# Graph network of four residual layers: source scales on GpSimd, chunk sums by an identity product and ScalarE

## Chip, cores and metric

The kernel runs on one core of a Trainium2 chip. The metric is the device time of one execution in microseconds (us), the median of several.

## What is computed

6250 nodes with 128 features, 206250 edges (sorted by destination, self loops among them), and four layers, each followed by `x = layernorm(x + layer(x))`:

```python
xw = x @ W0; ew = edge_attr @ edge_w
x = ln(x + segment_sum(xw[src] * ew, dst) + b0)                 # layer 0
agg = segment_sum(x[src], dst) / max(deg, 1)
x = ln(x + agg @ W_l.T + b_l + x @ W_r.T)                       # layer 1
norm = rsqrt(deg_src + eps)[src] * rsqrt(deg_dst + eps)[dst]
x = ln(x + segment_sum(x[src] * norm, dst) @ W2 + b2)           # layer 2
# layer 3: GCN sum, tanh, sigmoid gate, batch norm over all nodes
```

## The kernel before

Nodes lie in NB = 49 blocks of 128. A **loop** over 202 steps (about 95 to 2100 us) works through the edges: GpSimd gathers rows of `xw` by edge, TensorE and VectorE form layer 0's messages and sum them by node, and beside it TensorE and VectorE build the adjacency matrix, which is kept in DRAM as 196 float16 slices of 32 destinations each (`at`). As soon as blocks of layer 0 are final, the loop also normalises them, stores them as high and low float16 halves (`parts_v`, in `yT`), and already sums layer 1's neighbours with them: `acc` (which lies in `y`) holds features x destinations, in NCK = 14 **chunks** of CD = 448 columns. At the loop's end `DONE[c]` source blocks are in chunk c: 42, 45, 42, 42, 42, 42, 41, 42, 42, 42, 45, 45, 45, 45. The last NL = 4 blocks (LB = 45 on) are normalised only behind the loop.

The **stretch behind the loop** (2100 to 2164 us) finishes layer 1, and all that the change touches lies in it. There are two sizes: the 14 chunks c of 448 columns, and NCH = 13 chunks q of CB = 4 blocks (512 columns, the last one 128). `needs(q)` is the number of chunks c that q spans: 2, 3, 4, 5, 6, 7, 8, 10, 11, 12, 13, 14, 14.

- **TensorE** (`last_products`, L1489 on): for chunk c the products that are missing, two (high and low) for each source block from `DONE[c]` to 49, into PSUM bank `LAST_BANK[c % 4]`. Chunks 0 to 3 do the blocks below 45 first (18 products), then come the transposes and linear products of the last four blocks (L1520 to L1525), then chunks 0 to 13 to the end. Behind chunk c = `needs(q)` stands `y_linear(q)` (L1503): it waits for `needs(q)` chunks in `acc` and multiplies four blocks by the weights.
- **VectorE** (L1062 to L1122): `sum_out(i)` adds the bank of chunk i to `acc`. Between these stand the turns: turn q has `y_out(q)` (L1072, scale and add into `x`), `y_stats(q-1)` (L1081, L1085), `y_norm(q-2)` (L1093, L1095), `y_scaled(q-3)` (L1102: normalised rows times `src_l2` into `xs_c`) and `y_low(q-4)` (L1107: the low half for layer 2).
- **ScalarE** (L1752 on): turn q has the root for q (L1756), the normalised rows of q-1 into `y` (L1761, four instructions), and the cast of `xs_c` of q-2 to the high half (L1767).
- **GpSimd** (L781 on), done with its gathers: it adds layer 2's bias to `y`, chunk by chunk, once `xs_c` of the chunk is written (L784).
- **SyncE** loads the last adjacency pieces of each chunk c (L414) and the first chunks of the dense part (`chunk_in`, L429): the first waits for the ninth finished piece, the second for the fourteenth.

The **dense part** follows (layers 2 and 3, to the end): TensorE multiplies the halves of all 49 blocks by each adjacency chunk (`main`, L1569 and L1570). In its first chunk it waits before every fourth block b for `y_low(b // 4)`. Ahead of it TensorE has to be through with all `y_linear`, with a loaded flag and with a branch. All engines run their own queues in the order in which the program is written, tied by semaphores; there is no scheduler.

Of the kernel before, what the change touches and what calls it, by code (L numbers as in the profile page):

```python
# [16 lines left out]
ALU = mybir.AluOpType  # L17
# [5 lines left out]
D = 128  # L23
ED = 16
P = 128
NB = -(-N // P)
# [40 lines left out]
CB = CN // P  # L67
# [86 lines left out]
def build(nc, xT_d, x_d, ea_d, src_d, dst_d, next_d, edges_d, firstq_d, first16_d, half_d, w_d, vec_d, out_d):  # L154
    ctx = ExitStack()
    with ctx:
# [572 lines left out]
        def _(pool):  # L729
# [51 lines left out]
            for q in range(NCH):  # L781
                here = y[:, CB * q:min(CB * q + CB, NB), :]
                pool.wait_ge(s_w2["xs"], q + 1)
                nc.gpsimd.tensor_tensor(here, here, vecs[:, B_L2, :].unsqueeze(1).broadcast_to([P, min(CB, NB - CB * q), D]), ALU.add).then_inc(s_w2["yb"], 1)  # L784
# [36 lines left out]
        def _(v):  # L821
# [239 lines left out]

            def sum_out(i):  # L1062
                here = acc[:, CD * i:CD * i + CD]
                v.wait_ge(s_piece, i + 1)
                nc.vector.tensor_tensor(here, here, PB[:, LAST_BANK[i % 4], 0:CD], ALU.add).then_inc(s_acc, 1)

            def y_out(q):
# [20 lines left out]
            def chunk(a, q):  # L1088
                return a[:, CB * q:min(CB * q + CB, NB)]
# [6 lines left out]

            def y_scaled(q):
                nb = min(CB, NB - CB * q)
                v.wait_ge(s_w2["xn"], q + 1)
                if q >= 2:  # L1100
                    v.wait_ge(s_w2["lo"], q - 1)
                nc.vector.tensor_tensor(xs_c[q % 2][:, 0:nb, :], chunk(y, q), chunk(src_l2, q).unsqueeze(2).broadcast_to([P, nb, D]), ALU.mult).then_inc(s_w2["xs"], 1)  # L1102

            def y_low(q):
# [4 lines left out]
            def turn(q):  # L1109
                for step_of, behind in ((y_out, 0), (y_stats, 1), (y_norm, 2), (y_scaled, 3), (y_low, 4)):  # L1110
                    if 0 <= q - behind < NCH:
                        step_of(q - behind)

            q = 0
            for i in range(NCK):
                sum_out(i)
                while q < NCH and needs(q) <= i:
                    turn(q)
                    q += 1
            while q < NCH + 4:  # L1120
                turn(q)
                q += 1  # L1122

# [243 lines left out]
        def _(pe):  # L1367
# [121 lines left out]
            def last_products(c, b0, b1):  # L1489
                room, came, count = last_room(c)  # L1490
                bank = PB[:, LAST_BANK[c % 4], 0:CD]
                pe.wait_ge(s_part, NG1 + int(b1 > LB))
                pe.wait_ge(came, count)
                if c >= 4 and b0 == DONE[c]:
                    pe.wait_ge(s_acc, c - 3)
                a_piece = room[:, 0:CHJ * (NB - DONE[c]) * SN].rearrange("p (h n) -> p h n", h=CHJ).rearrange("p h (b d) -> p h b d", d=SN)
                for b in range(b0, b1):
                    for part_of in range(2):
                        last = nc.tensor.matmul(bank, parts_v[part_of][:, b, :], a_piece[:, :, b - DONE[c], :], start=(b == DONE[c] and part_of == 0), stop=(b == NB - 1 and part_of == 1))
                if b1 == NB:  # L1500
                    last.then_inc(s_piece, 1)
# [11 lines left out]
            pe.wait_ge(s_msg, 2 * NH)  # L1513
            pe.wait_ge(s_aev, 2 * NA)
            for c in range(4):
                if DONE[c] < LB:
                    last_products(c, DONE[c], LB)
            pe.wait_ge(s_lact, 2)
# [154 lines left out]
        def _(act):  # L1673
# [75 lines left out]
            nc.scalar.copy(xnT_l, PB[:, 3, 0:NL * P]).then_inc(s_lact, 1)  # L1749

            for at_turn in range(NCH + 2):
                q = at_turn  # L1752
                if q < NCH:
# [189 lines left out]
```

## Time and profile before

| | |
|---|---|
| median of 3 runs | 2810.82 us (2810.7 to 2816.72) |
| the profiled execution | 2810.7 us, span 2808.9 us |
| TensorE busy | 2238.8 us (80%) |
| VectorE busy | 1564.6 us (56%) |
| GpSimd busy | 1651.5 us (59%) |
| ScalarE busy | 498.4 us (18%) |
| loop | to 2100 us, held by gathers, TensorE and VectorE in turns |
| stretch behind the loop | 2100 to 2164 us |
| dense part | 2164 us to the end, TensorE without idle time for nearly all of it |

The span is from the first to the last instruction of one execution, and the engines' times are shares of it. Only what lies on the chain that ends last counts for the metric.

### The profile page before, as it was taken

The page shows a single profiled execution, that of the slowest core. Times are in us where ns is not written, and L with a number is a line of the kernel's source. Part 1 is how long each engine was busy: PE and PEld are TensorE (multiplying, and loading weights), DVE is VectorE, ACT ScalarE, POOL GpSimd, SP SyncE. Part 2 cuts the span into 40 slices and gives each one's busy share as a digit, 9 for nine tenths or more (in the row PEclk, how much of TensorE's full clock was granted, in tenths as well). Part 3 has the DMA queues.
Part 4 walks back from the last instruction along what each step waited for, and adds up shares of the span by engine and source line. Part 5 has one row for each costly group of instructions (what it writes and reads, how often), then busy time and mean ns, then how long its engine had stood idle before and what let it go on. Part 6 is the DMA issues. An engine that isn't in the chain of part 4 may idle for free.

```text
span 2808.9 us, 35420 instructions
## 1 busy us (share of the span) xinstructions
PE 2238.8 (80%) x13074; PEld 1423.0 (51%) x13074; DVE 1564.6 (56%) x2590; ACT 498.4 (18%) x798; POOL 1651.5 (59%) x1762
## 2 busy tenths in 40 slices
PE   4677777886787767787778787777778999999995
PEld 3455555554554545555555554544444444455553
DVE  3688888788887666666667664222228111212126
ACT  1122222222222111111212111000004111111113
POOL 4777777777777777777777777777762000012222
PEclk6566777778787777787878777777679999999998
DMA  7234443445455444554545557544447787776651
GB/s 231 82 110 127 124 136 123 137 142 141 140 153 153 125 141 127 143 148 129 168 141 154 153 152 145 152 127 112 100 124 245 261 290 276 259 287 247 246 200 46
DMA packets 456701, 456.24 MB, mean 162 GB/s; under 512 B 204789, under 2 KB 402250, under 8 KB 456522
## 3 DMA queue, kind: packets, MB, share of 16 engines
q1 hardware_dynamic: 212046, 271.95, 28.3%
q0 software_dynamic: 52832, 109.16, 14.7%
q10 hardware_dynamic: 191644, 72.77, 10.6%
q8 instruction: 109, 1.79, 0.3%
q14 instruction: 70, 0.57, 0.1%
HBM read 368.61 MB, written 85.13 MB: 162 GB/s over the span
## 4 chain that ended last, share of the span: by engine, by line
PE 45%; POOL 20%; issue 11%; DMA 11%; DVE 10%; ACT 1%; DVEq 1%; SPq 1%; POOLq 0%; ACTq 0%
POOL big L775 19%; PE pb L1465 11%; DMA big<-xw,big 10%; PE pb L1569 9%; PE pb L1570 9%; PE pb L1386 6%; DVE big L984 4%; PE pb L1438 3%; PE pb L1428 2%; PE pb L1444 2%; DVE big L888 2%; DVE big L890 1%; PE pb L1587 1%; DVEq L897 1%; ACT tmp L1696 1%
## 5 line engine op out<-in xcount | busy, mean ns | idle before, releaser
L775 POOL DMA_INDIRECT big<-xw,big x1612 | 1525.8, 947 | 528.8 <-issue 496.0
L1386 PE MATMUL pb<-big 64*128 64x512 f32 x808 | 310.1, 853 | 463.1 <-DVE big L984 460.0
L984 DVE TENSOR_TENSOR big<-pb,big 128x512 f32<-128x512 f32 x404 | 259.8, 685 | 702.6 <-DMA big<-xw,big 679.7
L1465 PEld LDWEIGHTS pb<-big 128*128 128x128 f32 x3232 | 539.5, 261 | 219.0 <-issue 170.7
L1465 PE MATMUL pb<-big 128*128 128x64 f32 x3232 | 572.5, 351 | 1.4 <-DVE big L984 1.4
L1696 ACT CAST tmp<-pb 128x784 f16<-128x784 f32 x392 | 318.3, 812 | 1310.0 <-PE pb L1438 1275.5
L888 DVE TENSOR_TENSOR big<-pb,big 128x2048 f16<-128x2048 f32 x196 | 447.1, 2281 | 0.8
L890 DVE TENSOR_TENSOR big<-pb,big 128x1568 f16<-128x1568 f32 x196 | 348.4, 1778 | 0.0
L1386 PEld LDWEIGHTS pb<-big 64*128 64x128 f32 x808 | 77.1, 233 | 502.2 <-DVE big L984 490.7
L1438 PE MATMUL pb<-big 128*128 128x98 f16 x3136 | 249.0, 232 | 45.4 <-ACT tmp L1696 28.9
L1438 PEld LDWEIGHTS pb<-big 128*128 128x128 f16 x3136 | 222.0, 117 | 106.1 <-issue 47.7
L1569 PE MATMUL pb<-big,x 128*128 128x512 f16 (+1 forms) x637 | 229.7, 369 | 6.5 <-issue 6.5
L1569 PE MATMUL pb<-big,yT 128*128 128x512 f16 (+1 forms) x637 | 230.2, 368 | 3.8 <-DMA big<-at 3.8
L1570 PE MATMUL pb<-big,yT 128*128 128x512 f16 (+1 forms) x637 | 230.2, 368 | 0.0
L1570 PE MATMUL pb<-big,x 128*128 128x512 f16 (+1 forms) x637 | 229.4, 368 | 0.0
L1428 PE MATMUL pb<-big,yT 128*128 128x448 f16 x910 | 219.2, 398 | 0.0
L1444 PE MATMUL pb<-tmp,ident 128*128 128x392 f16 x784 | 215.6, 411 | 0.0
L802 POOL TENSOR_TENSOR wts<-x 128x256 f32<-128x256 f32 x24 | 16.8, 723 | 246.5 <-DVE x L1266 246.5
L790 POOL MEMSET vecs<- 128x256 f32 x1 | 0.3, 312 | 271.0 <-DVE yT L1213 271.0
L1428 PEld LDWEIGHTS pb<-big,yT 128*128 128x128 f16 x910 | 101.4, 113 | 102.0 <-issue 44.5
L855 DVE TENSOR_TENSOR big<-pb,big 128x512 f32<-128x512 f32 x202 | 137.2, 679 | 0.0
L1194 DVE SCALAR_TENSOR_TENSOR y<-pb,small,y 128x128 f32<-128x128 f32 x49 | 13.9, 344 | 182.8 <-PE pb L1587 182.8
(230 smaller groups left out, 1639.7 us busy)
## 6 DMA issues: line engine op xcount, KB each, us to landing
at<-tmp SPq DMA_DIRECT2D x196, 392.0 KB
big<-at SPq DMA_DIRECT2D x24, 3200.0 KB, 11.2
big<-at SPq DMA_DIRECT2D x24, 3072.0 KB, 19.8
big<-xw,big POOLq DMA_INDIRECT x1612
big<-at ACTq DMA_DIRECT2D x22, 896.0 KB
big<-at ACTq DMA_DIRECT2D x27, 672.0 KB
big<-in_ea SPq DMA_DIRECT2D x202, 64.0 KB
tmp<-at ACTq DMA_DIRECT2D x9, 896.0 KB
```

The source lines that it names most:

```text
L775: nc.gpsimd.indirect_dma_start(gath[:, T8 * (n % NG) + t % T8, :], None, xw_d, bass.IndirectOffsetOnAxis(ap=src_i[:, t:t + 1], axis=0)).th ...
L888: nc.vector.tensor_tensor(hot_lo[:, at_pair:at_pair + NPR, :], cols[:, 0:P].unsqueeze(1).broadcast_to([P, NPR, P]), lokeyT[:, b % 3, c:c + ...
L890: last = nc.vector.tensor_tensor(hot_key[:, at_pair:at_pair + NPR, :], cols[:, P:P + KW].unsqueeze(1).broadcast_to([P, NPR, KW]), lokeyT[: ...
L984: nc.vector.tensor_tensor(msg[:, T8 * (n % 2) + 4 * q:T8 * (n % 2) + 4 * q + 4, :], PB[:, q, :].rearrange("p (t f) -> p t f", f=D), gath[: ...
L1386: last = nc.tensor.matmul(PB[:, q, :], ea[4 * ED * q:4 * ED * q + 4 * ED, n % NG, :], edge_w[4 * ED * q:4 * ED * q + 4 * ED, 4 * q:4 * q + ...
L1428: nc.tensor.matmul(bank, parts_v[part_of][:, b0 + b, :], a_piece[:, :, b, :], start=(b == 0 and part_of == 0), stop=(b == size - 1 and par ...
L1438: last = nc.tensor.matmul(PB[:, 4 + g, i * KW:i * KW + KW], hot_lo[:, at_pair, :], hot_key[:, at_pair, :], start=True, stop=True)
L1444: last = nc.tensor.matmul(PB[:, 6, 0:NB * T8], ident16[:, :], stage[:, j % 2, :].rearrange("p (h d) -> p h d", d=SN)[:, :, g * T8:g * T8 + ...
L1465: last = nc.tensor.matmul(PB[:, 2 + n % 2, 0:WIN], msg[:, T8 * (n % 2) + t, :], hot_win[:, T8 * (n % 2) + t, :], start=(t == 0), stop=(t = ...
L1569: nc.tensor.matmul(PB[:, c, 0:n], hi[:, b, :], piece, start=(b == 0), stop=False)
L1570: last = nc.tensor.matmul(PB[:, c, 0:n], lo[:, b, :], piece, start=False, stop=(k == 2 and b == NB - 1))
L1696: nc.scalar.copy(stage[:, j % 2, :].rearrange("p (h d) -> p h d", d=SN)[:, :, c:c + 4 * GP].rearrange("p h (k i a) -> p h k i a", k=2, a=2 ...
```

## The change

- VectorE loses `sum_out` and `y_scaled`. Its program is then 17 turns of four steps.
- The sum of what the loop left in `acc` and the last products is formed in PSUM: ahead of a chunk's products stands a product of the identity matrix with `acc` of the chunk, in float32, 448 columns (`start=True`), and all other products of the chunk add to it. For chunks 0 to 3 it stands in the first pass. TensorE waits once more for the loop's last jobs (`s_jev`).
- ScalarE copies the finished bank to `acc`: chunks 0 to 2 ahead of its turns, chunk t+3 at the head of turn t.
- GpSimd forms `y_scaled` ahead of its bias addition, waiting for ScalarE's normalised rows and, from the third chunk on, for VectorE's `y_low` of two chunks before.

```diff
@@ GpSimd
             for q in range(NCH):
                 here = y[:, CB * q:min(CB * q + CB, NB), :]
+                nb = min(CB, NB - CB * q)
+                pool.wait_ge(s_w2["xn"], q + 1)
+                if q >= 2:
+                    pool.wait_ge(s_w2["lo"], q - 1)
+                nc.gpsimd.tensor_tensor(xs_c[q % 2][:, 0:nb, :], here, src_l2[:, CB * q:CB * q + nb].unsqueeze(2).broadcast_to([P, nb, D]), ALU.mult).then_inc(s_w2["xs"], 1)
                 pool.wait_ge(s_w2["xs"], q + 1)
@@ VectorE
-            def sum_out(i):
-                here = acc[:, CD * i:CD * i + CD]
-                v.wait_ge(s_piece, i + 1)
-                nc.vector.tensor_tensor(here, here, PB[:, LAST_BANK[i % 4], 0:CD], ALU.add).then_inc(s_acc, 1)
...
-                for step_of, behind in ((y_out, 0), (y_stats, 1), (y_norm, 2), (y_scaled, 3), (y_low, 4)):
+                for step_of, behind in ((y_out, 0), (y_stats, 1), (y_norm, 2), (y_low, 4)):
...
-            q = 0
-            for i in range(NCK):
-                sum_out(i)
-                while q < NCH and needs(q) <= i:
-                    turn(q)
-                    q += 1
-            while q < NCH + 4:
+            for q in range(NCH + 4):
                 turn(q)
-                q += 1
@@ TensorE
-                if c >= 4 and b0 == DONE[c]:
-                    pe.wait_ge(s_acc, c - 3)
+                if c >= 4 or b1 == LB:
+                    if c >= 4:
+                        pe.wait_ge(s_acc, c - 3)
+                    nc.tensor.matmul(bank, ident[:, :], acc[:, CD * c:CD * c + CD], start=True, stop=False)
...
-                        last = nc.tensor.matmul(bank, parts_v[part_of][:, b, :], a_piece[:, :, b - DONE[c], :], start=(b == DONE[c] and part_of == 0), stop=(b == NB - 1 and part_of == 1))
+                        last = nc.tensor.matmul(bank, parts_v[part_of][:, b, :], a_piece[:, :, b - DONE[c], :], start=False, stop=(b == NB - 1 and part_of == 1))
...
+            pe.wait_ge(s_jev, evacs(NH))
             for c in range(4):
-                if DONE[c] < LB:
-                    last_products(c, DONE[c], LB)
+                last_products(c, DONE[c], LB)
@@ ScalarE
+            def sum_out(c):
+                act.wait_ge(s_piece, c + 1)
+                nc.scalar.copy(acc[:, CD * c:CD * c + CD], PB[:, LAST_BANK[c % 4], 0:CD]).then_inc(s_acc, 1)
+
+            for c in range(3):
+                sum_out(c)
             for at_turn in range(NCH + 2):
+                if at_turn + 3 < NCK:
+                    sum_out(at_turn + 3)
                 q = at_turn
```

On ScalarE a turn from the middle of the stretch, and the start of the next, read, before (`l1_stats` is VectorE's L1085, `walk2_norm` its L1095, `walk2_xs` its L1102):

```order
L1756 ACTIVATE rstd<-mean_var,eps_ln 128x4 [waits l1_stats]
L1761 ACTIVATE y<-x,shift,rstd 128x128 [waits walk2_norm]
L1761 ACTIVATE y<-x,shift,rstd 128x128 x3
L1767 CAST x<-tmp 128x4x128 [waits walk2_xs]
L1756 ACTIVATE rstd<-mean_var,eps_ln 128x4 [waits l1_stats]
```

and now:

```order
L1741 COPY y<-pb 128x448 [waits last_piece_done]
L1752 ACTIVATE rstd<-mean_var,eps_ln 128x4 [waits l1_stats]
L1757 ACTIVATE y<-x,shift,rstd 128x128 [waits walk2_norm]
L1757 ACTIVATE y<-x,shift,rstd 128x128 x3
L1763 CAST x<-tmp 128x4x128 [waits walk2_xs]
L1741 COPY y<-pb 128x448 [waits last_piece_done]
```

At the head of each turn there is now a copy (L1741) that waits for TensorE's finished chunk, and the root, the rows and the cast stand behind it; `walk2_xs` now comes from GpSimd.

On TensorE the end of the stretch read, before (chunks 12 and 13 and the last four linear steps; L1499 the chunk's products, L1510 `y_linear`; `last_acc_added` is the sum in `acc`):

```order
L1499 MATMUL pb<-big,yT 128x448 [waits last_acc_added,kept_in2,parts_ready]
L1499 MATMUL pb<-big,yT 128x448 x7
L1510 MATMUL pb<-wts,y 128x128 [waits l1_y,last_acc_added]
L1510 MATMUL pb<-wts,y 128x128 x3
L1499 MATMUL pb<-big,yT 128x448 [waits last_acc_added,ring_in1,parts_ready]
L1499 MATMUL pb<-big,yT 128x448 x7
L1510 MATMUL pb<-wts,y 128x128 [waits l1_y,last_acc_added]
L1510 MATMUL pb<-wts,y 128x128 x3
L1510 MATMUL pb<-wts,y 128x128 [waits l1_y,last_acc_added]
L1510 MATMUL pb<-wts,y 128x128 x3
L1510 MATMUL pb<-wts,y 128x128 [waits l1_y,last_acc_added]
```

and now, for the same chunks 12 and 13:

```order
L1483 MATMUL pb<-y,ident 128x448 [waits last_acc_added,kept_in2,parts_ready]
L1487 MATMUL pb<-big,yT 128x448 x8
L1498 MATMUL pb<-wts,y 128x128 [waits l1_y,last_acc_added]
L1498 MATMUL pb<-wts,y 128x128 x3
L1483 MATMUL pb<-y,ident 128x448 [waits last_acc_added,ring_in1,parts_ready]
L1487 MATMUL pb<-big,yT 128x448 x8
L1498 MATMUL pb<-wts,y 128x128 [waits l1_y,last_acc_added]
L1498 MATMUL pb<-wts,y 128x128 x3
L1498 MATMUL pb<-wts,y 128x128 [waits l1_y,last_acc_added]
L1498 MATMUL pb<-wts,y 128x128 x3
L1498 MATMUL pb<-wts,y 128x128 [waits l1_y,last_acc_added]
```

An identity product of 448 columns (L1483) stands ahead of each chunk's products (now L1487), and `last_acc_added` is now raised by ScalarE. The linear products keep their places.

On GpSimd the product of a chunk with the scales now stands ahead of the chunk's bias addition, thirteen pairs in a row; the product waits for ScalarE's rows (`walk2_xn`) and from the third on for VectorE's low half (`walk2_lo`).

## Rows read from the trace of the kernel before

**Rows 1.** Timeline, TensorE: start us, us, line, operation, tiles, count, [idle before it, releaser].

```profile
2101.34 4.50 PE L1499 MATMUL pb<-big,yT 128*128 128x448 f16 x18
2106.15 0.66 PE L1520 MATMUL pb<-ident,tmp 128*128 128x128 f32 x4 [0.31 <-ACT tmp L1744]
...
2109.38 4.70 PE L1499 MATMUL pb<-big,yT 128*128 128x448 f16 x24
2113.92 1.05 PE L1510 MATMUL pb<-wts,y 128*128 128x128 f32 x8
2114.81 1.68 PE L1499 MATMUL pb<-big,yT 128*128 128x448 f16 x8
...
2141.23 1.16 PE L1510 MATMUL pb<-wts,y 128*128 128x128 f32 x8 [1.62 <-DVE y L1065]
...
2155.26 2.50 PE L1510 MATMUL pb<-wts,y 128*128 128x128 f32 x10 [3.07 <-DVE y L1065]
2164.31 0.58 PE L1569 MATMUL pb<-big,x 128*128 128x512 f16 x1 [6.54 <-issue]
```

**Rows 2.** Timeline, VectorE, one turn; columns as before, and one start after an idle wait.

```profile
2136.34 0.61 DVE L1065 TENSOR_TENSOR y<-y,pb 128x448 f32<-128x448 f32 x1
2136.87 1.12 DVE L1072 SCALAR_TENSOR_TENSOR x<-pb,small,x 128x128 f32<-128x128 f32 x4
2137.91 0.86 DVE L1081 BATCH_NORM_STATS2 stats<-x 128x6 f32<-128x128 f32 x4
2138.80 0.38 DVE L1085 BATCH_NORM_AGGREGATE mean_var<-stats 128x2 f32<-128x6 f32 x4
...
2139.36 0.69 DVE L1102 TENSOR_TENSOR tmp<-y,small 128x512 f32<-128x512 f32 x1
2139.96 0.68 DVE L1107 TENSOR_TENSOR x<-tmp,x 128x512 f16<-128x512 f32 x1
2140.57 1.14 DVE L1065 TENSOR_TENSOR y<-y,pb 128x448 f32<-128x448 f32 x2
2142.43 1.13 DVE L1072 SCALAR_TENSOR_TENSOR x<-pb,small,x 128x128 f32<-128x128 f32 x4 [0.72 <-PE pb L1510]
```

**Rows 3.** Timeline, ScalarE: a copy of 512 columns, and one turn.

```profile
2106.85 0.59 ACT L1749 COPY tmp<-pb 128x512 f32<-128x512 f32 x1
...
2139.21 0.30 ACT L1756 ACTIVATE rstd<-mean_var,eps_ln 128x4 f32<-128x4 f32 x1 [1.81 <-DVE mean_var L1085]
2139.47 1.65 ACT L1761 ACTIVATE y<-x,shift,rstd 128x128 f32<-128x128 f32 x4
2141.03 0.60 ACT L1767 CAST x<-tmp 128x512 f16<-128x512 f32 x1
```

**Rows 4.** Timeline, GpSimd: the first bias addition, and one later.

```profile
2127.76 1.27 POOL L784 TENSOR_TENSOR y<-y,vecs 128x512 f32<-128x512 f32 x1 [34.03 <-DVE tmp L1102]
...
2140.12 1.66 POOL L784 TENSOR_TENSOR y<-y,vecs 128x512 f32<-128x512 f32 x1 [2.58 <-DVE tmp L1102]
```

**Rows 5.** Timeline, TensorE, at the end of the kernel: identity products, 512 and 384 columns.

```profile
2785.54 1.77 PE L1646 MATMUL pb<-y,ident 128*128 128x512 f32 x4 [0.23 <-DVE x L1354]
```

**Rows 6.** Busy time by microsecond; after GpSimd's stand granted clock, DMA share, GB/s.

```profile
2103.00:2104.00 1.00, 1.00 (x7) 0.43 (x5) 0.56 (x5) 0.29 (x1) 0.00 (x0) 0.89 0.00 0
...
2154.00:2155.00 1.00, 0.00 (x0) 0.00 (x0) 1.00 (x3) 1.00 (x3) 0.84 (x1) 0.71 1.06 386
...
2168.00:2169.00 1.00, 1.00 (x6) 0.43 (x5) 1.00 (x2) 0.86 (x2) 1.00 (x1) 0.96 1.02 376
```

**Rows 7.** Chain of waits, in order of time: start us, us, what.

```profile
2161.92 0.69 DVE x L1107
2162.61 1.70 issue
...
2168.47 0.22 PE pb L1569
```

**Rows 8.** DMA issues, 2085 to 2230 us: source, count, KB, median us to landing.

```profile
big<-at SPq DMA_DIRECT2D x4, 3072.0 KB, 19.9
```

More of the change, by code:

```diff
@@ L1095, in y_norm @@
                 nc.vector.scalar_tensor_tensor(out=chunk(shift, q), in0=chunk(mean_var, q)[:, :, 0], scalar=-1.0, in1=chunk(rstd, q), op0=ALU.mult, op1=ALU.mult).then_inc(s_w2["norm"], 1)
[L1097 to L1102, printed above, removed]
             def y_low(q):
```

## Prediction

> **What bounds the kernel now.** I read the timeline of TensorE first, from the end of the edge loop to the first product of the dense part, because every edit lies there. After the loop's last transposes TensorE runs 18 products on the first four chunks, waits 0.31 us for ScalarE's normalised rows, and from 2109.38 works without idle time for 30 us. Then `y_linear` rows have idle time before them that ends with a VectorE L1065, 1.62 us at 2141.23 and 3.07 us at 2155.26, the first and the last of four [rows 1]. So the stretch has two halves: TensorE sets the pace at first, VectorE later. VectorE's timeline says at what pace: one turn runs from 2136.34 to 2140.57, 4.23 us, of which L1065 takes 0.53 (2136.34 to 2136.87) and L1102 0.60 (2139.36 to 2139.96) [rows 2]; these two are what the change takes away. The stretch ends when the last `y_linear` ends at 2157.76 (2155.26 and 2.50); after 6.54 us that the profile calls issue, the dense part begins at 2164.31 [rows 1]. Behind that TensorE has its products in a row, so the time follows the end of the last `y_linear`.
>
> **TensorE's part.** One identity product of 448 float32 columns has no row of its own. A `y_linear` of 4 x 128 float32 columns moves TensorE on by 0.89 us (2113.92 to 2114.81) [rows 1], which gives 448 / 512 x 0.89 = 0.78 us; an identity product over 512 and one over 384 columns together take 1.77 us [rows 5], at most 0.88 us for half of it. I take 0.78. A float16 product of the pieces takes 4.54 / 24 = 0.189 us [rows 1].
>
> The first four identity products stand between 2101.34 and the transposes that were ready at 2106.15. The 18 products took 4.50 us and not 3.40, since the clock was at half (1.2 GHz) until some 2103.2, as the mean of 0.89 from 2103 on says [rows 1, 6]. The new walk: the first identity product 1.56 us at half clock, to 2102.9; six float16 products, the first still slow, 1.3, to 2104.2; then three identity products (2.34) and twelve float16 ones (2.27), to 2108.8. That is **+2.65 us**, and it shifts all that is behind (2.2 at the least, were the first one at full clock; 3.6 with 0.88 each). The later products start at 2112.0.
>
> I name the chunks c = 0 to 13 and the linear steps L0 to L12. From there to L7 TensorE has: 32 products of chunks 0 to 3 (6.05), 86 of chunks 4 to 9 (16.25) with six identity products (4.68), chunk 10 with 8 and one (2.29), and L0 to L6 at 0.89 (6.23), 35.5 us together. L7 starts at **2147.5** instead of 2141.23. VectorE no longer limits here: its turn is now 4.23 - 1.13 = 3.10 us, and a TensorE turn of 14 products, an identity product and a linear step is 2.65 + 0.78 + 0.89 = 4.32. That is already slower than the VectorE turn it replaces. Were this all, the rest (chunks 11 to 13, 24 products and three identity products, L7 to L12) takes 4.54 + 2.34 + 4.67 = 11.5 us and ends at 2159.1, 1.3 us late.
>
> **ScalarE's part, the wait that is added.** ScalarE copies chunk t+3 at the head of its turn t, and behind that copy stand the root of chunk t, the normalising of t-1 and the cast of t-2, in order. L0 to L6 need a copy that comes early, but the chunks of 448 columns and the linear steps of 512 don't keep step. L7 needs chunk 9, whose copy heads turn 6; by the round below it is there at 2140.9 (start of L6) + 6.59 = 2147.5, just in time. L8 needs chunk 10, whose copy heads turn 7, and turn 7 begins only when turn 6 is through. Turn 6 waits for the statistics of chunk 6, and VectorE takes these only behind its output of L7. So there is a **ring**: L7, VectorE, ScalarE's turn 6, the copy of chunk 10, L8, and the same for L9, L10 and L11 (chunks 11, 12, 13). One round from rows: start of a `y_linear` that was waited for to VectorE's L1072, 2141.23 to 2142.43, 1.20; L1072 to L1081 1.04 and to L1085 0.89 [rows 1, 2]; L1085 to ScalarE's root, 2138.80 to 2139.21, 0.41; root 0.26, normalising 1.56, cast 0.60 [rows 2, 3]; the copy. A copy of 448 columns on ScalarE isn't in the trace: 448 / 512 of the 0.59 us of L1749 is 0.52, and VectorE's own L1065 0.61 is the other end [rows 2, 3]; with 0.1 us to reach TensorE I take 0.63. The round is 1.20 + 1.04 + 0.89 + 0.41 + 0.26 + 1.56 + 0.60 + 0.63 = **6.59 us**, where the turns took 4.23.
>
> L8 starts at 2147.5 + 6.59 = 2154.1, L9 at 2160.7, L10 at 2167.3, L11 at 2173.9, and L12 (one block, the same copy) ends 0.89 + 0.22 later, at 2175.0. Against 2157.76 that is +17.2 us. TensorE's own work in a round (0.89 + 0.78 + 1.51) fits into it.
>
> The clock is on top. In the kernel before it fell to half within 2154 to 2155 and was back within 2168 to 2169, 4 us after the dense part had begun [rows 6]; its L11 and L12 took 2.50 us [rows 1]. In the new one TensorE has some 3.4 us idle in each round from 2151 on. An idle stretch of 3.07 us was followed by half clock before [rows 1, 6], so I take L10 at half (+0.9) and L11 with L12 (+1.1): +2.0. The ends are 0 and +3.8 (L8 and L9 too). **The last `y_linear` ends at 2177.0, +19.2 us.**
>
> **GpSimd's part.** A product of 128 x 512 with the scales is not in the trace; the addition of the same size takes 1.27 us once and 1.66 us in the other turns [rows 4]. A chunk costs GpSimd then 2.5 to 3.3 us beside a ring of 6.6 or TensorE turns of 4.3: it waits for ScalarE, not the other way. In the turn shown, VectorE's L1107 takes 0.68 us while GpSimd's addition at 2140.12 overlaps it, no longer than L1102 ahead of it [rows 2, 4]; what stretches is the addition, by 0.39 us. So I cost VectorE at its old durations.
>
> **What stays hidden.** The dense part needs the low halves chunk by chunk, 8 products a chunk at 0.22 us [rows 7]: it begins at 2177.0 + 6.5 = 2183.5 and reaches the last chunk at 2183.5 + 96 x 0.22 + 1.8 for the slow start, 2206.4. The last low half comes about three turns after L12: 3 x 2.4 us of ScalarE plus VectorE and GpSimd's 3.3, near 2191. The loads of the dense part wait for pieces: the first for the ninth, which TensorE ends near 2141; a half took 19.9 us to land [rows 8], so to 2161, ahead of 2183.5. The second load waits for the fourteenth piece, whose products stand behind L9 and end near 2164; 20 us later is 2184, ahead of its use at 2206. Both cost nothing. The 6.54 us of issue I keep (it lay in a stretch full of loads, and will again); if it shrank to the 1.7 us that the chain of waits charges as issue behind a VectorE step [rows 7], 4.8 us come off.
>
> **The rivals.** *TensorE alone decides* (the ring doesn't close, since ScalarE's copies come early enough): last `y_linear` at 2159.1, 2812 us. For it: TensorE is without idle time over the first 30 us. Against it: the copy heads a turn that waits for VectorE, by the order of the program. It would need a round under 3.2 us. *Faster:* if the start of the dense part were bound by VectorE's chain, as the chain of waits reads it (an L1107 ends at 2162.6, then 1.7 us of issue) [rows 7], taking 13 x 1.13 us off VectorE would start it earlier; TensorE's own sum with the first identity products under ScalarE's wait ends at 2156.5, and with 1.7 us of issue behind it the dense part begins 6.1 us earlier, 2804.7. It decides only where the ring is shorter than TensorE's 3.2 us. Against it: the first product of the dense part needs only the first low half, and L1107 rows stand from before 2140 on [rows 2]. *GpSimd decides:* L2 starts near 2123.2, and 5.36 us of the round later, at 2128.6, GpSimd has its first chunk. With p us for each of its operations the last low half comes at 2128.6 + 12 x 2p + p + 0.6, which is behind 2206.4 from p = 3.1 on; at 4 us it is 2229.2, 22.8 us late, 2853. Against it: 1.66 us for the addition, which has a broadcast input too [rows 4]. *GpSimd and VectorE shut each other out:* if L1107 waited for both GpSimd operations of a turn, VectorE's turn would be 3.10 + 2 x 1.66 = 6.42 us. The ring has room for that (VectorE is needed in it for 2.3 us of 6.59), but the three turns before L7 that hold an L1107 would be 6.42 - 4.32 = 2.1 us longer, 6.3 us together: 2836.3. Against it: the 0.68 us beside an addition [rows 2, 4]. The Trainium skill (SBUF — State Buffer, section SBUF: two separate sides) has such a rule: a VectorE instruction with two SBUF inputs and a GpSimd instruction that reads SBUF take a shared port pair as an exclusive lock, for the whole instruction. By that rule this rival holds; the stretch of 0.39 us on GpSimd alone is all that the rows show of it. *The change doesn't do what it says:* if VectorE kept its two steps, its turns of 4.23 us would stay, and 2811; the order shows them gone from it, so I set no chance aside.
>
> **How the numbers follow.** The profiled execution took 2810.7 us, and the median of the runs is 2810.82: 2810.8 + 19.2 = **2830.0**. The ends of its terms: 0 to +3.8 of clock (from +2.0 taken), -0.5 to +1.0 of the first products, +-0.3 us in each of four rounds, -4.8 to +1.5 of issue: 2822 to 2836, and the run-to-run width widens it to 2821 to 2838. Chances: the ring 0.80 (2821 to 2838), 0.04 of it with the two engines shutting each other out (2836); TensorE alone 0.09 (2812); faster 0.04 (2805); GpSimd or a clock that stays low into the dense part 0.07 (over 2838). The ring's range alone holds eight in ten. A measurement of this kernel can tell about 0.2% (5.6 us) from no change: faster 0.04, within 0.09, slower 0.87.
>
> **What would show it.** In the profile after: identity products of about 0.78 us ahead of each chunk; L7 near 2147; then `y_linear` rows each with idle time ended by ScalarE's copy, 6 to 7.5 us apart; a copy that starts right behind a ScalarE cast and long after its piece was done; VectorE idle in each round, ended by TensorE; the dense part beginning near 2183. Wrong would be the prediction if the `y_linear` rows from L8 on followed at 3 to 4 us, if idle time in the dense part were ended by low halves, or if the last `y_linear` ended before 2170.

## The result

The changed kernel is slower: 2832.24 us (2829.51 to 2835.67, 6 runs) beside 2817.09 us for the kernel before in the same comparison (2810.7 to 2819.3, 6 runs). The ratio is **1.0061, 95% interval 1.005 to 1.0071**, or +17.2 us on 2817 (the two medians are 15.2 us apart). The prediction was 2830.0, +19.2 us on 2810.8.

The two profiled executions differ by 21.5 us in span (2808.9 and 2830.4), and 3.5 us of this lie ahead of every edit: the last transposes of the loop start at 2100.43 before and at 2103.97 after. In the traces of this case the loop ends between 2094.8 and 2105.4 us, whatever the kernel, so total times scatter, while the time behind the loop repeats: 57.33 us to the end of the last `y_linear` in the kernel before, and 57.33 in an experiment that leaves this part as it was. What still varies is TensorE's clock at its start. In the six kernels that do the first identity products and then the same 24 products on TensorE, the 24 begin 11.5 to 12.8 us behind the transposes: in the latest (12.77, the first experiment) the granted clock is back from half to full 5.5 us behind the transposes, in the changed kernel (11.75) 3.5 us. So stretches that differ by about 1 us need a look at the clock. Because the totals scatter, all readings below are taken from the start of these transposes: the **stretch** to the end of the last `y_linear` is 57.3 us before and 75.3 after, and the dense part begins at +63.9 and at +81.3. Those 17.4 us are the result; what is left of the 21.5 is 0.6 us in the dense part, where a wait for a load between 2400 and 2500 us is 4.8 us instead of 3.8.

The timeline of TensorE after the change (columns as in rows 1; L1483 is the identity product, L1487 the products of the pieces, L1498 `y_linear`, L1557 the dense part):

```profile
2103.97 1.10 PE L1473 MATMUL pb<-ident,yT 128*128 128x128 f32 x4 [0.42 <-DVE yT L907]
...
2115.72 4.70 PE L1487 MATMUL pb<-big,yT 128*128 128x448 f16 x24
...
2123.56 0.92 PE L1483 MATMUL pb<-y,ident 128*128 128x448 f32 x2
2124.31 2.81 PE L1487 MATMUL pb<-big,yT 128*128 128x448 f16 x14
...
2151.07 1.05 PE L1498 MATMUL pb<-wts,y 128*128 128x128 f32 x8
...
2152.71 1.68 PE L1487 MATMUL pb<-big,yT 128*128 128x448 f16 x8
2157.41 1.16 PE L1498 MATMUL pb<-wts,y 128*128 128x128 f32 x8 [3.02 <-ACT y L1741]
...
2170.29 1.16 PE L1498 MATMUL pb<-wts,y 128*128 128x128 f32 x8 [3.02 <-ACT y L1741]
2176.74 2.50 PE L1498 MATMUL pb<-wts,y 128*128 128x128 f32 x10 [5.29 <-ACT y L1741]
2185.25 0.59 PE L1557 MATMUL pb<-big,x 128*128 128x512 f16 x1 [6.01 <-DVE x L1100]
```

The identity product of 448 columns moves TensorE on by 0.75 us (2123.56 to 2124.31). The 24 products at 2109.38 in [rows 1], 8.95 us behind the transposes, start at 2115.72 here, 11.75 behind them: 2.8 us later. L7 starts at 2151.07, which is +47.1; the row at 2141.23 in [rows 1] is +40.8. From L8 on, each `y_linear` (L9's row, at 2163.85, is in the chain below) has idle time before it that ends with ScalarE's L1741, the copy, and they stand 6.34, 6.44, 6.44 and 6.45 us apart. In [rows 1] it was VectorE's L1065.

The chain of waits between L8 and L9 shows the ring of the prediction link by link (start us, us, what):

```profile
2157.41 1.17 PE pb L1498 x8
...
2158.88 0.86 DVE x L1072 x3
2159.73 0.79 DVE stats L1081 x4
...
2160.54 0.39 DVE mean_var L1085 x4
...
2160.96 0.30 ACT rstd L1752
2161.26 1.61 ACT y L1757 x4
2162.87 0.51 ACT x L1763
2163.37 0.44 ACT y L1741
...
2163.85 1.17 PE pb L1498 x8
```

TensorE's linear step, three links on VectorE, four on ScalarE, and the next linear step: 2157.41 to 2163.85. No link is TensorE's identity product. The ends of ScalarE's turn, to be held against [rows 3]:

```profile
2160.96 0.30 ACT L1752 ACTIVATE rstd<-mean_var,eps_ln 128x4 f32<-128x4 f32 x1 [3.60 <-DVE mean_var L1085]
...
2163.28 0.52 ACT L1741 COPY y<-pb 128x448 f32<-128x448 f32 x1
```

The root waited 3.60 us for VectorE's L1085, and then root, rows, cast and copy run back to back, with the copy last in line. The piece that it copies had been done long before: chunk 11's products ran from 2152.71 to 2154.4, and its copy starts at 2163.28.

### The profile page after: what moved, and what is told of

It is laid out like the page before. It is cut to its first block, busy times and chain, and to the rows that moved or that the text cites. A ratio compares the mean times of both kernels' runs of the same rounds, so it can differ in the third digit from the quotient of the medians.

```text
span 2830.4 us, 35477 instructions
## 1 busy us (share of the span) xinstructions
PE 2250.8 (80%) x13102; PEld 1422.5 (50%) x13102; DVE 1552.5 (55%) x2563; ACT 504.7 (18%) x812; POOL 1663.5 (59%) x1775
## 4 chain that ended last, share of the span: by engine, by line
PE 47%; POOL 18%; DMA 11%; issue 11%; DVE 10%; ACT 1%; DVEq 1%; SPq 1%; POOLq 0%; ACTq 0%
POOL big L775 18%; PE pb L1451 12%; DMA big<-xw,big 10%; PE pb L1557 9%; PE pb L1558 9%; PE pb L1372 6%; DVE big L989 4%; PE pb L1424 3%; PE pb L1414 2%; DVE big L893 2%; PE pb L1430 2%; DVE big L895 2%; PE pb L1487 1%; PE pb L1575 1%; DVEq L902 1%
## 5 line engine op out<-in xcount | busy, mean ns | idle before, releaser
L1451 PEld LDWEIGHTS pb<-big 128*128 128x128 f32 x3232 | 533.5, 258 | 220.4 <-issue 172.6
L1451 PE MATMUL pb<-big 128*128 128x64 f32 x3232 | 566.3, 348 | 1.4 <-DVE big L989 1.4
L1557 PE MATMUL pb<-big,x 128*128 128x512 f16 (+1 forms) x637 | 229.8, 369 | 6.0 <-DVE x L1100 6.0
L1557 PE MATMUL pb<-big,yT 128*128 128x512 f16 (+1 forms) x637 | 230.0, 368 | 4.8 <-DMA big<-at 4.8
L1414 PE MATMUL pb<-big,yT 128*128 128x448 f16 x910 | 227.0, 408 | 0.0
```

The source lines that it names most:

```text
L1414: nc.tensor.matmul(bank, parts_v[part_of][:, b0 + b, :], a_piece[:, :, b, :], start=(b == 0 and part_of == 0), stop=(b == size - 1 and par ...
L1451: last = nc.tensor.matmul(PB[:, 2 + n % 2, 0:WIN], msg[:, T8 * (n % 2) + t, :], hot_win[:, T8 * (n % 2) + t, :], start=(t == 0), stop=(t = ...
L1557: nc.tensor.matmul(PB[:, c, 0:n], hi[:, b, :], piece, start=(b == 0), stop=False)
```

## Experiments

The theory: the copies on ScalarE, each behind a full turn, close a ring of 6.4 us. The rivals: TensorE's added products, GpSimd's added products, ScalarE's load as such.

**Copies one chunk earlier.** The changed kernel with:

```diff
-            for c in range(3):
+            for c in range(4):
                 sum_out(c)
             for at_turn in range(NCH + 2):
-                if at_turn + 3 < NCK:
-                    sum_out(at_turn + 3)
+                if at_turn + 4 < NCK:
+                    sum_out(at_turn + 4)
```

> The changed kernel, with ScalarE's copies one chunk earlier: chunks 0 to 3 ahead of the turns, chunk t+4 at the head of turn t. The measure is the stretch from the start of the loop's last transposes to the end of the last y_linear, 57.3 us before and 75.3 after. Ring theory (each of L8 to L11 waits for a copy behind a whole ScalarE turn that itself waits for the linear step before): the copy for L8 now heads a turn that needs only L7's predecessor, two linear steps share one round of 6.4 us, so 3.2 us for each, which is TensorE's own work; L8 to L10 start without idle time, the stretch is 62 to 64 us, and the kernel is 11 to 13 us faster than the changed one, 4 to 7 us slower than before. Rival, TensorE's added products are the cause: nothing is taken from TensorE, so the stretch stays near 75 us and the time at +17. Rival, ScalarE's added work of 0.52 us a turn is the cause: it stays as well, +17.

Measured: ratio 1.0025 (1.0015 to 1.0036), stretch 64.6 us. The same instructions on the same engines, and 10.6 of the 18 us are gone: the place of the copies in ScalarE's queue is the cause of most of it, not their load and not TensorE's. The stretch came out 0.6 us above the range that was expected. L7 is 1.0 us later than in the changed kernel (+48.1), by the clock at the start, and TensorE's timeline shows a second excess behind it:

```profile
2153.52 1.05 PE L1498 MATMUL pb<-wts,y 128*128 128x128 f32 x8
...
2159.86 1.16 PE L1498 MATMUL pb<-wts,y 128*128 128x128 f32 x8
...
2164.03 1.16 PE L1498 MATMUL pb<-wts,y 128*128 128x128 f32 x8 [0.74 <-ACT y L1741]
2168.19 1.84 PE L1498 MATMUL pb<-wts,y 128*128 128x128 f32 x10 [3.00 <-ACT y L1741]
```

L8 (left out here) and L9 follow L7 at TensorE's own pace (3.16 and 3.18 us), but L10 and L11 come 4.17 and 4.16 us apart (the last row, 1.84 us where the changed kernel has 2.50, gives 0.7 us back). In these rounds a small VectorE instruction, `shift` (L1095, four columns, two inputs in SBUF), took 1.17 us instead of 0.16. Beside it, GpSimd's bias addition:

```profile
2160.18 1.17 DVE L1095 SCALAR_TENSOR_TENSOR shift<-mean_var,rstd 128x4 f32<-128x4 f32 x1
```

```profile
2160.07 1.27 POOL L789 TENSOR_TENSOR y<-y,vecs 128x512 f32<-128x512 f32 x1
```

VectorE's ends at 2161.35, GpSimd's at 2161.34.

**Only the identity products.** The kernel before, TensorE as in the change, VectorE copies (`tensor_copy`) where it added; nothing on ScalarE or GpSimd.

> The kernel before with the identity products alone: TensorE adds the loop's sums, VectorE copies the bank to acc where it added it before, and the scales stay on VectorE. Ring theory: no ScalarE copy, so no ring; what is left is the 2.8 us of the first four products and TensorE turns of 4.3 us up to L7 (6.3 us late), of which VectorE's turns of 4.23 us get nothing back: stretch 63 to 65 us, +5 to +7.5 us against before. Rival, TensorE's added products are the whole cause: +17, stretch 75. Rival, the products are hidden: 0.

Measured: ratio 1.0021 (1.0011 to 1.0032), stretch 63.1 us, L7 at +46.9 and the next steps 3.16, 3.16, 3.38 and 4.23 us apart. TensorE's share of the cost is these 5.8 us of stretch. VectorE is not relieved here, since its copy takes the 0.62 us of the addition. From L7 to L11 it is 13.93 us in this kernel and 25.67 in the changed one: the ring's share is these 11.7 us.

**Only the scales.** The kernel before, with the product on GpSimd.

> The kernel before with the scales on GpSimd alone; sums stay on VectorE. VectorE's turn goes from 4.23 to 3.63 us and TensorE's turn without identity product is 3.54. My theory: the end of the stretch comes 3 to 4 us earlier (53.5 to 54.5 us for 57.3), the kernel is 3 to 4 us faster than before, at the edge of what can be told, and GpSimd's product takes 1.04 us as in the changed kernel. Rival, GpSimd's reads and VectorE's L1107 lock each other out in the tighter turns: VectorE's low halves get longer than 0.68 us, the gain shrinks to 0 or turns into 1 to 3 us of loss.

Measured: ratio 0.9996 (0.9986 to 1.0005), stretch 56.6 us: 0.7 us gained, not 3 to 4. The rival was right that VectorE is held, but about another instruction. VectorE, ScalarE and GpSimd in one turn (L1100 is `shift` here, L1759 ScalarE's rows, L787 and L789 GpSimd's product and addition):

```profile
2151.75 0.70 DVE L1100 SCALAR_TENSOR_TENSOR shift<-mean_var,rstd 128x4 f32<-128x4 f32 x1
...
2155.91 0.70 DVE L1100 SCALAR_TENSOR_TENSOR shift<-mean_var,rstd 128x4 f32<-128x4 f32 x1
```

```profile
2152.49 1.65 ACT L1759 ACTIVATE y<-x,shift,rstd 128x128 f32<-128x128 f32 x4 [0.50 <-DVE shift L1100]
```

```profile
2154.21 1.04 POOL L787 TENSOR_TENSOR tmp<-y,small 128x512 f32<-128x512 f32 x1 [1.78 <-ACT y L1759]
2155.33 1.26 POOL L789 TENSOR_TENSOR y<-y,vecs 128x512 f32<-128x512 f32 x1
```

`shift` takes 0.70 us, to 2156.61, and the addition that began at 2155.33 ends at 2156.59. Then ScalarE's rows wait for `shift`, GpSimd's product for the rows, the addition for the product, and the next `shift` for the addition: 2151.75 to 2155.91 is a round of 4.16 us, in place of the 3.63 us of VectorE's own work. A second ring, closed not by a semaphore but by two engines that can't read at the same time. The Trainium skill (SBUF — State Buffer, section SBUF: two separate sides) states the rule that was a rival in the prediction: a VectorE instruction with two inputs in SBUF and a GpSimd instruction that reads SBUF exclude each other for a whole instruction, and whoever starts first holds the other. The trace agrees, to 0.02 us.

**The scales back on VectorE.** The changed kernel without its GpSimd part.

> The changed kernel with the scales back on VectorE: only the sums are changed. Ring theory: VectorE has over 3 us of idle time in each round and the scales are not in it, so all y_linear rows from L8 on keep their spacing of 6.4 us, the stretch is 75 us, and the kernel is 17 us slower than before, like the changed one (within 1 us). Rival, moving the scales to GpSimd costs part of the 17 us: then this one is faster than the changed kernel by that part. Rival, VectorE's relief was worth something in the changed kernel: then this one is slower by 0.6 us for each round, 2 to 7 us.

Measured: ratio 1.007 (1.0053 to 1.0087), stretch 76.7 us, `y_linear` 6.34, 6.44, 6.45 and 7.36 us apart. Moving the scales to GpSimd costs the changed kernel nothing, and earns it nothing either. The stretch is 1.4 us above the changed kernel's (75 us were expected): 0.5 arises before the first linear step, by the clock, and 0.9 in L10 at half clock (2.08 us for 1.16), which made the last round longer.

**Additions last.** The kernel with only the scales on GpSimd (the `shift` ring above), with

```diff
-                pool.wait_ge(s_w2["xs"], q + 1)
+            pool.wait_ge(s_w2["xs"], NCH)
+            for q in range(NCH):
+                here = y[:, CB * q:min(CB * q + CB, NB), :]
                 nc.gpsimd.tensor_tensor(here, here, vecs[:, B_L2, :].unsqueeze(1).broadcast_to([P, min(CB, NB - CB * q), D]), ALU.add).then_inc(s_w2["yb"], 1)
```

> The kernel before with the scales on GpSimd (as the third run) and GpSimd's thirteen bias additions behind all its products. In the third run VectorE's shift (L1100, two inputs in SBUF) took 0.70 us for 0.16 and ended with GpSimd's addition each time, which closed a round of 4.16 us: addition, shift, ScalarE's rows, GpSimd's product, addition. Lock theory: without the addition in the round the shift is back at 0.16 us, VectorE's turn is the 3.63 us first expected, and the stretch from the loop's last transposes to the last y_linear ends at 54 to 55 us (57.4 before, 56.6 in the third run), 2 us or more earlier than in the third run. Rival, the shift waits for something of ScalarE or for VectorE's own order, and only by chance ends with the addition: the shift stays at 0.70 us and the turns at 4.16.

Measured: ratio 0.9983 (0.9972 to 0.9994), stretch 53.5 us. VectorE's `shift` (L1102) and GpSimd's products:

```profile
2152.18 0.16 DVE L1102 SCALAR_TENSOR_TENSOR shift<-mean_var,rstd 128x4 f32<-128x4 f32 x1
```

```profile
2150.49 1.04 POOL L787 TENSOR_TENSOR tmp<-y,small 128x512 f32<-128x512 f32 x1 [2.58 <-ACT y L1761]
2154.11 1.04 POOL L787 TENSOR_TENSOR tmp<-y,small 128x512 f32<-128x512 f32 x1 [2.58 <-ACT y L1761]
```

`shift` is back at 0.16 us, and the turn from product to product is 3.62 us, what VectorE's own work adds up to. The product alone keeps clear of `shift`. With this the second ring is shown from both sides: the addition in it 4.16 us, without it 3.62. (The clock cost 0.5 us at the start and gave back 0.6 in the last row, 1.89 us; the run with all three below has the same rounds and a stretch of 53.7.)

**Copies earlier and additions last.** Both repairs on the changed kernel.

> The changed kernel with ScalarE's copies one chunk earlier (as the first run) and GpSimd's additions behind all its products. The first run had 64.6 us of stretch, of which the last two linear steps came 4.17 us apart, and the shift took 1.17 to 1.24 us, ending with the addition. Lock theory: the linear steps from L8 on come 3.2 us apart (TensorE's own work), all at full clock but perhaps the last, so the stretch is 61 to 62.5 us, 2 to 3.5 us less than in the first run, and the kernel is 4 to 5 us slower than before. Rival, ScalarE's turn with the copy is what set 4.17: it stays, 64.6 us.

Measured: ratio 1.0022 (1.0011 to 1.0032), stretch 61.1 us.

```profile
2145.35 1.05 PE L1500 MATMUL pb<-wts,y 128*128 128x128 f32 x8
...
2154.95 1.06 PE L1500 MATMUL pb<-wts,y 128*128 128x128 f32 x8
2158.14 1.38 PE L1500 MATMUL pb<-wts,y 128*128 128x128 f32 x10 [2.13 <-ACT y L1743]
```

The linear steps, of which L8 and L9 are left out above, come 3.16 to 3.26 us apart to the end. L7 is 6.1 us late against before, TensorE's part. The rounds from L7 to L11 give back 1.2 us, and the last row, at full clock, 1.1 (1.38 us for 2.50); 3.7 us of stretch remain. The change repaired in its own terms is still slower than the kernel before.

**Identity product for chunks 10 to 13 alone.** The kernel with the additions last, and the identity product with ScalarE's copy (four chunks ahead) for the last four chunks.

> A version meant to beat both: scales on GpSimd, additions last, and the identity product with ScalarE's copy only for chunks 10 to 13, where TensorE has time, the copies four chunks ahead of the turn; chunks 0 to 9 stay on VectorE. If the ring and the lock are the only costs, L8 to L11 come 3.2 us apart, VectorE's turn is 3.1 us there, and the stretch is 52.5 to 54 us, 3.5 to 5 us less than before; the kernel is 3 to 5 us (0.1 to 0.2%) faster than before, and 1 to 2 us faster than with the additions last alone. Rival, TensorE's added products on any chunk cost what they take (4 x 0.76 us): no better than with the additions last alone, or worse by 1 to 2 us.

Measured: ratio 0.9989 (0.9978 to 1.0), stretch 54.0 us against 53.5 without it; the ratios don't tell the two apart. The steps of TensorE do, and the rival holds: TensorE has no time to spare there after all. From L6 to L7, where chunk 10's identity product stands, it is 5.80 us instead of 5.05. Behind that TensorE's round (0.89 + 0.75 + 1.51) is 3.2 us: the steps from L7 to L11 are 3.16, 3.23, 3.23 and 3.23 us apart instead of 2.48, 2.45, 3.62 and 3.62, 0.7 us more in all.

**Second load later.** The kernel before, with one wait on SyncE:

```diff
             general_sync(sp, 2, g_off)
+            sp.wait_ge(s_w2["lo"], 10)
             chunk_in(sp, 1)
```

> The kernel before with one wait more on SyncE: the second load of the dense part is issued only after VectorE's tenth low half (about 2165 us). It measures the issue time of 6.5 us between the last y_linear and the first product of the dense part, which I kept in the sum. Theory A, TensorE fetches its next instructions past the branch and shares the DMA with the load: with the DMA idle from 2156 on, the time shrinks to 2 to 4 us, and the kernel is up to 4 us faster (or the second chunk arrives late and takes part of it back). Theory B, the time is the flag's load and the branch itself, whatever the DMA does: it stays at 5 to 6.5 us, and the kernel is the same or, by the late load, slower.

Measured: ratio 0.9988 (0.9978 to 0.9998). The stretch is the same, 57.33 us, but the dense part begins at +60.8:

```profile
2149.65 2.50 PE L1511 MATMUL pb<-wts,y 128*128 128x128 f32 x10 [3.07 <-DVE y L1066]
2155.63 0.58 PE L1570 MATMUL pb<-big,x 128*128 128x512 f16 x1 [3.48 <-issue]
```

The idle time called issue is 3.48 us instead of the 6.54 of [rows 1]. What the DMA did meanwhile (busy times by microsecond as in rows 6; the last three numbers are clock, DMA share, GB/s), here and in the kernel before:

```profile
2153.00:2154.00 1.00, 0.00 (x0) 0.00 (x0) 1.00 (x5) 1.00 (x3) 1.00 (x1) 0.50 0.00 0
```

```profile
2159.00:2160.00 1.00, 0.00 (x0) 0.00 (x0) 1.00 (x5) 0.89 (x2) 1.00 (x1) 0.50 1.11 400
```

With the DMA idle, 3.1 us of the waiting go. But the load alone doesn't set the size of the wait: it is 4.9 us in the kernel with the scales back and in the one with the copies doubled (below), beside loads at over 375 GB/s all the time, and 7.20 us in the one with both repairs. The profile has a DMA queue for instructions, q8, which moves packets of 0.02 MB within this wait. Here, from 2152.15 to 2155.63, and in the kernel with doubled copies, from 2176.26 to 2181.18 (queue: packets, MB, share of the DMA engines):

```profile
q8 instruction: 1, 0.02, 2.4%
```

```profile
2181.18 0.58 PE L1558 MATMUL pb<-big,x 128*128 128x512 f16 x1 [4.92 <-issue]
```

```profile
q8 instruction: 1, 0.02, 1.4%
```

In the eight kernels with one such packet the dense part begins 2.7 to 3.0 us behind it. The packet starts 0.4 us behind the last `y_linear` here, with the DMA idle, and 2.1 to 3.8 us behind it beside a load. That fits a fetch of TensorE's next instructions, behind the branch, that shares the DMA with the load. Four kernels (before, the changed one, both repairs, all three together) have two packets and begin 3.2 to 4.3 us behind the second; why there are two, and what the 3 us behind the packet are, stays open. The second chunk arrived in time: TensorE has no further wait up to 2240 us.

**All three together.** Scales on GpSimd, additions last, second load behind the eighth low half.

> The kernel before with the three findings put together: scales on GpSimd, bias additions last, and the second load of the dense part issued behind VectorE's eighth low half. The parts were measured alone: the stretch from the loop's last transposes to the last y_linear fell from 57.4 to 53.5 us with the first two, and the time from there to the dense part's first product from 6.5 to 3.5 us with the third. If they add up, the dense part starts 57 us after the transposes instead of 63.9, and the kernel is 6 to 7.5 us (0.21 to 0.27%) faster than before. Rival: the second chunk's load, now later against an earlier dense part, arrives after TensorE wants it (22 us into the dense part), and part of the 7 us comes back there.

Measured: 2803.18 us, ratio **0.9983** (0.9974 to 0.9992), 4.8 us less than before and not the 6 to 7.5 that were expected. The dense part begins at +58.6, not 57:

```profile
2148.67 2.50 PE L1511 MATMUL pb<-wts,y 128*128 128x128 f32 x10 [2.46 <-DVE y L1073]
2156.07 0.58 PE L1570 MATMUL pb<-big,x 128*128 128x512 f16 x1 [4.90 <-issue]
```

The issue time is 4.9 us and not 3.5. The first chunk's load ran until 2151.7, only 0.5 us past the last linear step, so it can't account for all of the difference; this kernel has two instruction packets (2151.4 and 2151.8) where the one with the later load alone has one, and whether that is the cause is not shown. In the ratio it is no better than the additions last alone (0.9983 both); the 1.5 us by which its dense part begins earlier is below what these runs can tell.

**Copy twice.** The changed kernel with a second ScalarE copy of the same size ahead of each.

> The changed kernel with one more ScalarE copy of the same size, to unused space, ahead of each copy to acc (14 x 0.52 us of ScalarE, nothing on TensorE). Ring theory: each of the four rounds (L8 to L11) grows by the copy, from 6.44 to 6.96 us, so the stretch grows by 2.1 us, 2.6 if L7 is held as well, from 75.2 to 77.3 to 77.9, and the L steps before L7 stay where they are. Rival, TensorE's added products decide: ScalarE has idle time of 3 us and more in each round, the stretch stays at 75.2.

Measured: ratio 1.0073 (1.0058 to 1.0088), stretch 78.7 us. L7 to L12 (L1499 is `y_linear` here):

```profile
2144.77 1.16 PE L1499 MATMUL pb<-wts,y 128*128 128x128 f32 x8
...
2151.64 1.75 PE L1499 MATMUL pb<-wts,y 128*128 128x128 f32 x8 [3.44 <-ACT y L1744]
...
2159.10 2.08 PE L1499 MATMUL pb<-wts,y 128*128 128x128 f32 x8 [2.36 <-ACT y L1744]
...
2166.89 1.16 PE L1499 MATMUL pb<-wts,y 128*128 128x128 f32 x8 [2.84 <-ACT y L1744]
2173.76 2.50 PE L1499 MATMUL pb<-wts,y 128*128 128x128 f32 x10 [5.71 <-ACT y L1744]
```

0.43 us more ScalarE work, the copy's own pace, makes a round of 6.87 us where it was 6.45 (L10 to L11; L7 to L8 it was 6.34, with an L7 that had not been waited for), while ScalarE has 3.6 us of idle time or more in each round. The two other rounds are longer by another 0.6 and 0.9 us, and their linear steps took 1.75 and 2.08 us, wholly or in part at half clock; so the stretch is 0.8 us above the range that was expected. L0 to L6 stand where they did, within 0.1 us. Work on an engine that is idle half of the time lengthened the rounds at full clock one for one, because it lies in the ring. The ratio alone would not show it: its interval overlaps that of the changed kernel.

## Why the prediction was right, step by step

- **The first identity products**, +2.65 us: measured +2.8. Right, with 0.75 us for a product instead of 0.78 (the row that it was scaled from was close enough).
- **L7 6.3 us late**: measured 6.3 (+47.1 for +40.8). The only-TensorE run has the same L7 (+46.9), so this part is TensorE's alone.
- **The ring**: there, on the engines and in the order of the prediction, for L8 to L11. Its size was 6.59 us and is 6.44. The links from rows were right to 0.01 us (1.20, 1.04, 0.89, 0.42, 0.26, 1.55); the cast was taken at its duration, 0.60, where its pace to the next instruction is 0.51, and copy and way to TensorE take 0.57 and not 0.63.
- **The clock**, +2.0 us: L11 and L12 ran at half clock (2.50 us, as before), L10 did not (1.16), so the 0.9 us for it were not there. The clock did fall after the idle time at 2154 to 2157, but while TensorE did chunk 12's products, off the ring, and it was back by 2163:

```profile
2159.00:2160.00 1.00, 1.00 (x3) 0.21 (x2) 1.00 (x5) 0.00 (x0) 0.00 (x0) 0.50 1.07 390
2163.00:2164.00 1.00, 0.15 (x1) 0.15 (x2) 0.00 (x0) 0.80 (x2) 0.99 (x1) 1.00 1.07 390
2173.00:2174.00 1.00, 0.00 (x0) 0.00 (x0) 0.93 (x10) 0.16 (x1) 0.00 (x0) 0.50 1.06 405
```

  (granted clock 0.50, 1.00 and 0.50, behind GpSimd's column). The 1.1 us for L11 and L12 were right: the same ten products took 1.38 us in the run with both repairs, where the clock fell only as they ended. But the sum counts 0.89 + 0.22 = 1.11 us for them at full clock, 0.3 less than that row. Less 0.9 of clock and 0.7 of ring over four rounds, and 0.3 more for the last row, the 19.2 become the 17.9 measured.
- **GpSimd in the shadow**: right, up to the last `y_linear`. Its product takes 1.04 us, less than the addition:

```profile
2156.50 1.04 POOL L787 TENSOR_TENSOR tmp<-y,small 128x512 f32<-128x512 f32 x1 [4.17 <-ACT y L1757]
2157.62 1.27 POOL L789 TENSOR_TENSOR y<-y,vecs 128x512 f32<-128x512 f32 x1
...
2183.18 1.04 POOL L787 TENSOR_TENSOR tmp<-y,small 128x512 f32<-128x512 f32 x1 [4.97 <-ACT y L1757]
2184.30 1.67 POOL L789 TENSOR_TENSOR y<-y,vecs 128x512 f32<-128x512 f32 x1
```

  The addition takes 1.27 us when alone, and 1.67 when VectorE's instructions with two SBUF inputs fall into it (2184.30). So the 1.27 of [rows 4] was the undisturbed time and the 1.66 a held one. The prediction read this as the only effect that the rows show, and gave VectorE's old durations; in the changed kernel that was enough, since the ring leaves VectorE idle, and the lock first counted where the ring was gone.
- **The rest hidden**: right; once it has begun, the dense part has no wait up to 2240 us, neither for a low half nor for a load. The 6.5 us of issue were 6.0. The row at 2185.25 puts them down to VectorE's L1100, the low half that had ended last; but of the low halves that product waits only for the first chunk's, written by the L1100 at 2139.51, and in other kernels with the same wait the profile says issue.
- **The rivals**: TensorE alone would have been +1.3 us. The runs without a ring came out at 5.8 (VectorE copies) and 3.7 (both repairs). So this rival had too low a price even where the ring is gone: L11 waits for the copy of the last chunk, 2.13 us of idle time in the run with both repairs, or for VectorE's. The rival in which GpSimd and VectorE shut each other out had its place wrong (L1107 instead of `shift`), and applied in the kernels without the ring.

That the predicted time came within 2.2 us of the measured one is in part luck: the median of the kernel before was 6.3 us above the value that the prediction built on, and the two medians lie 4.0 us closer together than the 19.2. What bears the mechanism out is the stretch, +17.9 us for +19.2, and its links.

Why the change doesn't pay even without the ring: it takes 1.13 us a turn off VectorE, which bounds only the last third of the stretch, and adds 0.75 to TensorE, which bounds the first two thirds.

## To carry to other kernels

When a step moves to another engine's queue, ask not how busy that engine is but what stands ahead of it in the queue and whom that waits for; if the answer leads back to the step's own consumer, the sum of the links is the new pace. Such a ring is cut by issuing the step one turn earlier, and it is told from load by that (10.6 us came back with not one instruction fewer). And of two engines whose reads exclude each other, the small instruction on the path counts: keep the long one out of the round.

## What the runs showed of the hardware

- A VectorE `scalar_tensor_tensor` of four columns with both inputs in SBUF took 0.63 to 1.24 us for 0.16 when a GpSimd instruction that reads SBUF was under way, and ended within 0.02 us of it. It turned a gain of 3.8 us into 0.7.
- GpSimd's product of 128 x 512 with a broadcast scale takes 1.04 us, its addition of a broadcast row 1.27, and 1.66 when VectorE held it; VectorE took 0.69 for the product (0.60 to its next instruction).
- The pause of TensorE at the branch ahead of the dense part was 4.9 to 7.2 us in ten kernels with a load beside it, 4.9 in one where the load ended 0.5 us into it, and 3.5 in one with the DMA idle. Where the profile shows one instruction packet in the pause, the dense part begins 2.7 to 3.0 us behind it. A load that is issued earlier than it is needed can delay the engine that it serves.
